# Turned rows and left operands loaded by ScalarE's queue, x and labels by SyncE's, label loads paced

## The reference, cut to what matters

```python
q1 = _attn_pool(x, mask, w1, b1, w2)          # softmax over the 50 rows of exp((x w1 + b1) w2)
q2 = _attn_pool(x, mask, w3, b3, w4)
h = jnp.concatenate([q1, q2], axis=1) @ w5 + b5
f6 = h @ w6 + b6
g = (v @ v.T)[iu, ju]                          # iu, ju: the 44850 pairs i < j
cross = h[:, iu] * h[:, ju] * g
f7 = cross @ w7 + b7
out8 = jnp.concatenate([f6, f7], axis=1) @ w8 + b8
return jnp.einsum('bu,bku->bk', out8, label_embedding)
```

## Time and profile before

| | |
|---|---|
| time, three runs | 1756.97, 1757.58 (median), 1764.65 us |
| profiled execution | 1763.27 us, its span 1761.5 us |
| mean granted TensorE clock | 0.969 of full speed |
| data moved by DMA | 615.20 MB, 349 GB/s over the span |

### The profile page before, as it was taken

The page is one execution under the profiler, slowest core; times in us unless marked ns, Lnnn a source line. Parts: engine busy times, 40 slices in busy tenths (PEclk is TensorE's granted clock), DMA queues, the critical chain, the costliest instruction groups (busy, mean ns, idle before and its releaser), DMA issues.

```text
span 1761.5 us, 25362 instructions
## 1 busy us (share of the span) xinstructions
PE 1580.9 (90%) x7096; PEld 1158.8 (66%) x7096; DVE 1428.3 (81%) x5487; ACT 996.4 (57%) x2931; POOL 138.0 (8%) x96
## 2 busy tenths in 40 slices
PE   1899999999999999999999999989999999997700
PEld 0566677677777777777776777757777777765500
DVE  8997888873898999799997986747777667679966
ACT  7665777765564646464655644434444444433497
POOL 5000000000000000000000000000000000003366
PEclk9999999999999999999999999999999999999955
DMA  7799876977899999999999898999999989999898
GB/s 294 263 401 357 286 274 238 336 268 241 311 329 390 362 400 354 412 374 362 394 355 389 313 389 312 371 414 407 352 379 375 336 309 409 352 356 406 341 397 361
DMA packets 170385, 615.20 MB, mean 349 GB/s; under 512 B 20784, under 2 KB 49421, under 8 KB 162053
## 3 DMA queue, kind: packets, MB, share of 16 engines
q1 hardware_dynamic: 106469, 368.44, 54.8%
q10 hardware_dynamic: 61696, 242.33, 37.0%
q0 software_dynamic: 2080, 2.81, 0.5%
HBM read 609.70 MB, written 3.79 MB: 348 GB/s over the span
## 4 chain that ended last, share of the span: by engine, by line
PE 67%; DMA 14%; DVE 12%; ACT 5%; issue 1%; ACTq 0%; POOL 0%; SPq 0%; DVEq 0%; POOLq 0%
PE bank L704 61%; DMA wring<-in_w7p 8%; DVE stream L1072 4%; DVE cring L1051 3%; DVE junk L951 3%; PE bank L654 2%; DMA stream<-in_label 2%; ACT stream L871 2%; DMA stream<-in_x 2%; PE bank L669 2%; DMA sring<-hrows 1%; ACT absjunk L769 1%; ACT wring L860 1%; ACT stage L871 1%; PE bank L689 1%
## 5 line engine op out<-in xcount | busy, mean ns | idle before, releaser
L704 PE MATMUL bank<-wring,cring 128*128 128x300 f32 (+1 forms) x5616 | 1444.0, 418 | 41.4 <-DVE cring L1051 15.3
L704 PEld LDWEIGHTS bank<-wring,cring 128*128 128x128 f32 (+1 forms) x5616 | 1062.2, 190 | 407.2 <-issue 32.6
L860 ACT ACTIVATE wring<-wring,gcol 128x300 f32<-128x300 f32 x1403 | 655.4, 534 | 675.1 <-PE bank L704 583.5
L1051 DVE TENSOR_TENSOR cring<-lefts,sring 128x1024 f32<-128x1024 f32 (+2 forms) x312 | 371.9, 1192 | 183.3 <-PE bank L704 157.4
L1072 DVE SCALAR_TENSOR_TENSOR stream<-stream,out 128x300 f32<-128x300 f32 x1080 | 441.8, 466 | 0.5 <-DMA stream<-in_label 0.5
L951 DVE SCALAR_TENSOR_TENSOR junk<-stream,ubc 128x300 bf16<-128x300 f32 x784 | 320.1, 466 | 31.9 <-DMA stream<-in_x 31.9
L769 ACT ACTIVATE absjunk<-stream 128x300 bf16<-128x300 f32 x448 | 196.0, 439 | 14.4 <-DMA stream<-in_x 8.9
L654 PE MATMUL bank<-stream,stage 128*32 128x300 f32 x896 | 63.9, 438 | 37.0 <-DVE small L993 36.4
L1072 DVE DVE_READ_ACCUMULATOR stream<-stream,out 128x1 f32 x1080 | 89.0, 82 | 0.0
L769 ACT ACTIVATION_READ_ACCUMULATOR absjunk<-stream 128x1 f32 x448 | 83.9, 187 | 0.0
L1072 DVE SCALAR_TENSOR_TENSOR stream<-stream,bank 128x300 f32<-128x300 f32 x160 | 64.8, 461 | 22.1 <-DMA stream<-in_label 22.1
(11 more groups left out here) (88 smaller groups left out, 516.7 us busy)
## 6 DMA issues: line engine op xcount, KB each, us to landing
wring<-in_w7p ACTq DMA_DIRECT2D x365, 600.0 KB, 7.4
stream<-in_label SPq DMA_DIRECT2D x276, 750.0 KB, 10.1
stream<-in_x SPq DMA_DIRECT2D x64, 1050.0 KB, 11.9
sring<-hrows SPq DMA_DIRECT2D x152, 256.0 KB
stage<-in_label SPq DMA_DIRECT2D x44, 750.0 KB, 9.2
wring<-in_w7p ACTq DMA_DIRECT2D x18, 450.0 KB, 4.6
wring<-in_w7p ACTq DMA_DIRECT2D x18, 300.0 KB, 6.7
sring<-hrows SPq DMA_DIRECT2D x96, 44.0 KB
```

What stands on the lines that cost most here:

```text
L704: mm = pe.matmul(acc[b % 4][:, 0:E], cring[0:rows, p % CSLOTS, b % 2, j0 + j, :], w, start=(p == BEGIN[b] and j == 0), stop=(p == END[b] - ...
L860: ins = nc.scalar.activation(w, w, ACT.Copy, scale=gcol[:, t:t + 1])
L1051: nc.vector.tensor_tensor(cut(cring, p % CSLOTS, j0), in0, cut(sring, nb % SSLOTS, j0), ALU.mult).then_inc(c_ready, 1)
```

## The change

The functions `s_load` and `left_load` move, unchanged but for the engine, from SyncE's program to ScalarE's. On ScalarE `s_load` stands behind `w7_load` and ahead of `w7_scale` in its step, and `left_load` behind `w7_scale`. The loads for the first units, which SyncE had at step 0, stand at the end of ScalarE's step -1. SyncE keeps `x`, labels, constants and the last results. The label plan loses its three-step distance: a new slot is free at once (the four that lie where constants were, at `H_DONE` = 248), and no load is placed less than two steps behind the third load ahead of it. By the code, 32 of the 320 loads get another step: seven early ones move from steps 100 to 105 to 99 to 104, and loads 134 to 158, which stood at 246 to 268, stand at 247 to 267, three in two steps at most.

```diff
-    assert X_DONE + 3 * (FIRST_LATE - NARROW) > DOTS[NS - 1][1] + LATE[H_OUT]
+    H_DONE = DOTS[NS - 1][1] + LATE[H_OUT] + 1
...
         free = (L_END[L_BEFORE[n]] if L_BEFORE[n] is not None else
-                X_WIDE_DONE + n if n < NARROW else X_DONE + 3 * (L_SLOT[n] - NARROW))
-        L_LOAD.append(max(free, L_LOAD[-1] if n else free))
+                X_WIDE_DONE if n < NARROW else H_DONE if L_SLOT[n] >= FIRST_LATE else X_DONE)
+
+        L_LOAD.append(max([free] + L_LOAD[-1:] + [q + 2 for q in L_LOAD[-3:-2]]))
+    assert all(a < z for a, z in zip(L_LOAD, L_END))
...
             for q in range(START, STOP):
-                if q == 0:
-                    s_load(0)
-                    left_load(0)
-                    s_load(1)
                 for n in [n for n in range(XSLOTS, NS * PARTS) if x_load_step(n) == q]:
                     x_load(n)
-                if q == 0:
-                    for n in range(2, SSLOTS):
-                        s_load(n)
-                if 0 <= q < POS:
-                    for n in BUFFERS:
-                        if NU * (n // BUFS) + LAST_USE[n % BUFS] == q and n + SSLOTS in BUFFERS:
-                            sp.wait_ge(c_ready, q + 1)
-                            s_load(n + SSLOTS)
-                    for b in whole(H_OUT, q - STORED):
-                        if b >= 1:
-                            left_load(b)
                 for n in [n for n in range(NBT * LC) if L_LOAD[n] == q]:
                     l_load(n)
...
                 if 0 <= q < POS:
                     if q + WSLOTS - 1 < POS:
                         w7_load(q + WSLOTS - 1)
+                    for n in BUFFERS:
+                        if NU * (n // BUFS) + LAST_USE[n % BUFS] == q and n + SSLOTS in BUFFERS:
+                            act.wait_ge(c_ready, q + 1)
+                            s_load(n + SSLOTS)
                     if q + AHEAD < POS:
                         w7_scale(q + AHEAD)
+                for b in whole(H_OUT, q - STORED):
+                    if b >= 1:
+                        left_load(b)
...
                 if q == -1:
                     for p in range(AHEAD):
                         w7_scale(p)
+                    s_load(0)
+                    left_load(0)
+                    for n in range(1, SSLOTS):
+                        s_load(n)
```

More of the change, by code:

```diff
@@ L451, in l_load @@
                 sp.dma_start(lring[L_SLOT[n]], label_v[n // LC, :, n % LC]).then_inc(l_in[L_SLOT[n]], 16)
[L453 to L506, removed]
@@ L845, in out8_done, with turned, left_load @@
                 act.sem_inc(out8_ready, 1)
+            def turned(b, row, pitch, rows, tiles):
+                return bass.AP(hrows[b].tensor, row * P, [[P, rows], [pitch * P, tiles], [1, P]])
+            def left_load(b):
+                if b >= 4:
+                    act.wait_ge(c_ready, END[b - 4])
+                act.wait_ge(a_stored[b], 16 * 2)
+                for name in ("A32", "A64"):
+                    row = A0 + int(name[1:])
+                    act.dma_start(left_of(name, b), hrows[b][row:row + P]).then_inc(lefta_in[b], 16)
+                act.wait_ge(bc_stored[b], 16 * 4)
+                for name in ("B32", "B64", "B96"):
+                    row = B0 + int(name[1:])
+                    act.dma_start(left_of(name, b), hrows[b][row:row + P]).then_inc(leftb_in[b], 16)
+                four = bass.AP(hrows[b].tensor, C0 * P, [[0, 4], [P, 32], [1, P]])
+                act.dma_start(left_of("C", b), four).then_inc(leftb_in[b], 16)
@@ new lines, in s_load @@
+            def s_load(n):
+                kind, own = KINDS[n % BUFS]
+                s = s_in[n % SSLOTS]
+                for b in live_at(n):
+                    tiles = sring[:, n % SSLOTS, b % 2]
+                    act.wait_ge(a_stored[b], 16 * 2)
+                    if kind != "A":
+                        act.wait_ge(bc_stored[b], 16 * 4)
+                    if kind == "D":
+                        act.wait_ge(d_stored[b], 16 * 2)
+                    if kind in ("A", "B", "D"):
+                        row = {"A": A0, "B": B0, "D": D0}[kind] + QUAD * own
+                        src = bass.AP(hrows[b].tensor, row * P, [[P, P], [1, QUAD * P]])
+                        act.dma_start(tiles.rearrange("p j l -> p (j l)"), src).then_inc(s, 16)
+                        continue
+                    for side in range(2):
+                        j0, ni = 2 * side, CUSTOM[own]
+                        if own == 4:
+                            for r in range(4):
+                                row = C0 + 40 + r + (0 if side else 3)
+                                src = bass.AP(hrows[b].tensor, row * P, [[0 if side else 3 * P, 7], [1, P]])
+                                act.dma_start(tiles[7 * r:7 * r + 7, j0, :], src).then_inc(s, 16)
+                            row = C0 + (0 if side else 22)
+                            act.dma_start(tiles[28:LAST_ROWS, j0, :], hrows[b][row:row + 22]).then_inc(s, 16)
+                            continue
+                        if own == 0:
+                            half = 0 if side else 64
+                            act.dma_start(tiles[0:64, j0, :], hrows[b][A0 + half:A0 + half + 64]).then_inc(s, 16)
+                            act.dma_start(tiles[64:P, j0, :], hrows[b][B0 + half:B0 + half + 64]).then_inc(s, 16)
+                            j0, ni = j0 + 1, 1
+                        i0 = max(0, 2 * own - 1)
+                        for k, (r0, r1) in enumerate(((0, REST), (REST, 2 * REST), (2 * REST, P))):
+                            src = turned(b, C0, 0, r1 - r0, ni) if side else turned(b, C0 + 3 * i0 + 1 + k, 3, r1 - r0, ni)
+                            act.dma_start(tiles[r0:r1, j0:j0 + ni, :], src).then_inc(s, 16)
```

## The result

The changed kernel takes 1845.3 us (median of 4 runs, 1841.8 to 1849.0) against 1760.6 us for the kernel before on the same chip (4 runs, 1757.0 to 1764.7): ratio 1.0475, 95% interval 1.0455 to 1.0495. That is 85 us slower, where 12 to 15 had been forecast. The profiled execution took 1846.9 us, its span is 1845.1 us and its granted clock 0.950 (before: span 1761.5 us, clock 0.969).

What follows compares the result with a forecast made beforehand. The prediction took TensorE to bound the middle and DMA both ends. Its terms, +28.5 - 8.7 - 3 - 2 = +14.8 us, on the 1757.6 us median gave 1772 us, with an 8-in-10 range of 1745 to 1790.

Steps and rivals of the forecast that it cites:

- Together 9.6 + 2.7 + 16.2 = 28.5 us, bounds 0 and 30: Part 1, turned rows issued by ScalarE: TensorE's loss at own0 (9.6), own3 (2.7) and own4 (16.2 us).
- lost one for one: 180 to 1558 us, TensorE-bound: whatever makes TensorE wait costs equal time; some 16 us were to be won.
- own1 and own2: nothing, the cover is thin: Steps loading own1 and own2: 6.9 us of ScalarE work against 8.08, so no loss, with 1.1 us of cover.
- The upper bound of 30: Part 1, issues on ScalarE: the most they could cost, at full issue time, with SyncE's times taken for ScalarE.
- The model of the hold: ScalarE's steps: 5.8 us between weight load and scaling are free, each us beyond is TensorE's; own0 4.4 us each.
- Both alone would do: Hole at 1153 us, step 268: pacing the labels or moving turned rows would each close it, gaining 8.7 us.
- The two medians of the earlier trace: Same 60 us near step 268: label loads landed in 22.9 us, ScalarE's weight loads in 7.8; queues don't hold each other.
- First stage −3: Part 3, tile 0 alone: earlier x loads gain more than late start and own0 cost; 3 us gained, bounds -6 and +4.
- Waits for x −2: Part 4, VectorE's 32.7 us of waits for x: x lands sooner, 2 us gained, bounds -6 and 0.
- hidden issues: Rival: ScalarE's issues cost TensorE nothing, so 1744 us; chance 0.25.
- half the price: Rival: a small piece's issue on ScalarE takes 0.25 us, so 1753 us; chance 0.14.
- ScalarE's queue becomes the late one: Rival: turned rows hold up weights in their shared queue, another 8 to 20 us, 1780 to 1792 us; chance 0.08.

Runs made afterwards that it cites:

- e5: Kernel before with the new label plan and only the own buffers issued by ScalarE, the other turned rows and left operands by SyncE: 1833.0 us, ratio 1.0391.
- e9: Changed kernel with each own buffer loaded as one DMA a tile, 128 runs of 2 KB, other rows of h: 1767.1 us, ratio 1.0027.
- e13: As e9, but each own load split by partitions into 10 or 6 issues a tile, still 2 KB runs: 1836.8 us, ratio 1.0429.
- e16: As e9, with 14, 6 or 12 wasted copies a tile on ScalarE behind each own load, holding ScalarE as long as e13's pieces: 1806.8 us, ratio 1.0260.
- e1: Kernel before with the new label plan alone, turned rows and left operands still on SyncE: 1758.4 us, ratio 0.9988.
- e2: Changed kernel with the old label plan, a burst of 18 label loads in step 268: 1843.9 us, ratio 1.0473.
- e12: Kernel before with the new label plan; GpSimd issues turned rows and left operands between steps 42 and 371, SyncE in the other steps: 1754.7 us, ratio 0.9960.
- e7: Changed kernel with SyncE keeping its old waits for h and for VectorE, empty, so early x loads go out late: 1850.2 us, ratio 1.0493.
- e11: Changed kernel with own buffers and left operands back on SyncE, only kinds A, B, D on ScalarE: 1770.5 us, ratio 1.0047.
- e3: Changed kernel with only the own buffers back on SyncE, kinds A, B, D and left operands on ScalarE: 1782.6 us, ratio 1.0121.
- e10: Changed kernel with at most four own pieces issued a step, spread over three or five steps, same queue: 1816.9 us, ratio 1.0314.

## Why the prediction was wrong

The direction was right and so was its first cause: ScalarE's issues delay the scaling and TensorE waits for it. The size was wrong by a factor of six, outside the range. By the terms of the sum:

- **"Together 9.6 + 2.7 + 16.2 = 28.5 us, bounds 0 and 30" is the step that failed.** The own buffers alone cost 69 us (e5), or 79 against a single load a tile (e9). Three things are missing in it. First the clock: a long hole costs some 2 us more than its wait, and TensorE's busy time rose by 27.5 us in all; I had priced waits alone ("lost one for one"), though the hole of the earlier trace rows, a wait of 8.72, is worth 10.5 when it goes. Second the shared queue: 30 us (e13 less e16), of which weights that land late behind the pieces are the part that rows show; I had left this to a rival. Third the length of the issues where short runs meet full queues: 12.4 and 12.6 us for own1 and own3 in place of 4.7. It is why "own1 and own2: nothing, the cover is thin" failed at steps 124 and 217, 9 and 11 us, and why own3 lost 9.4 us at step 150 in place of 0.9. With long runs these three holes are gone, but two of late weights stand near steps 128 and 221, so that the net is 8 us: the stretched issue and the late weight stand in for each other, and no run parts them.
- The upper bound of 30, hardly above the term itself, was set at the full issue time *as seen on a quiet SyncE queue*. The two issues of the earlier trace rows that took 6.21 us were against it, and so was a row of the trace of before that I passed over, own3's twelve pieces of step 150:

```profile
648.20 20.85 SPq L506 DMA_DIRECT2D sring<-hrows  x12
```

  Taken as the bound (20.85 + 0.38 + 1.85 against 6.06) that step alone would have lost 17 us in place of 0.9, which puts the upper end at 1806 us by this step alone.
- **The model of the hold held.** With matched holds and no pieces in the queue (e16) the holes are 4.56 and 4.42 us at own0 (worked out: 4.4 each), 0.80 us in step 200 with its mixing (worked out: 0.8), 0.88 and 0.95 us at own3 of steps 150 and 336 (worked out: 0.9) and 4.8 us at each of own4's three (3.5, 5.6 and 7.1 were worked out, 5.4 in the mean; that the mean comes near is in part luck).
- **"Both alone would do" was half wrong.** The pacing alone only moves the hole (e1); the queue alone closes it (e2 and the changed kernel, step 277). The gain was 10.5 us, not 8.7. The two medians of the earlier trace rows had it right: what is behind in one queue does not hold the other. The Trainium skill ("DMA: Bandwidth & Descriptors", section "Issuing engines are not separate DMA queues") says that issuing from several engines only saves the sequencer's time. The runs do not agree: another queue closed the hole (e2, ratio 1.0473 against 1.0475 with the pacing), as did GpSimd's (e12), and pacing in the same queue did not (e1, 0.9988); the times of the earlier trace rows run from the issue on, so no sequencer's time is in them.
- **First stage −3:** it lost 13.8 us by step 42. The `x` loads went out at once, three at 62.17 us, and e7 shows 7 us of gain from it. The DMA share from 78 to 178 us fell from 0.98 to 0.89, so the side of the term that counted bandwidth held. The late start is not what failed either: I had taken 2.5 us for it, and at step 1 the kernel is 3.4 us behind. The loss comes behind it. TensorE's waits for scaling between 60 and 200 us rose from 2.1 to 12.8 us, the longest, 4.8 us, at own0 of step 14 (worked out: 2.4). But e9 and e11 lose 10 to 12 us by step 42 with one issue a tile, or with the own buffers on SyncE. What costs them that stays open.

```profile
62.17 1.36 SPq L443 DMA_DIRECT2D stream<-in_x  x3
```

- **Waits for x −2:** VectorE's wait fell from 32.7 us to 8.7, and no time came with it, since TensorE wasn't waiting there.

```profile
DVE junk L948 <- DMA stream<-in_x: 8.7, 5, 3.4
```

Of the rivals, hidden issues and half the price are refuted by the rows of steps 107 and 124. The one that I gave least, "ScalarE's queue becomes the late one", was true as well, on top of the forecast: e13's weights, issued three units ahead, landed in 20.8 us near step 128 and not in 7.8, where e9's took 14.2. I had read its price off the burst of the earlier trace rows, in which there were no pieces in the weights' own queue.

A rival to "the queue" is that the two engines' issues wait for something that both share, since SyncE's issues are long in the same moments (four label loads in 10.49 us from 571.95 us on, in the changed kernel). The kernel before speaks against it. While SyncE's two issues took 6.21 us, those of the weights on ScalarE, six between 1151 and 1172 us (shortest, median, longest in ns), took

```profile
L852 ACTq DMA_DIRECT2D wring<-in_w7p x6: 334/334/367, 1151.3 to 1171.5; - x6
```

What stays open: how the pieces in ScalarE's queue delay the weights behind them, when an issue is stretched and when the load behind is late in its place, and why one load of weights in e9 took 12.12 us to issue. e13's pieces are as large in sum as e9's loads. And the matching of the holds in e16 is good to about 0.6 us a place, so the split of 41 and 30 is no finer than its intervals.

## What to carry to other kernels

Don't put many small DMAs on the queue and the engine that feed the bounding engine: here they cost by the time they held the engine, by loads behind them that came late, and by the clock after each hole. Price an issue by the longest row of its kind, not by one from a quiet stretch, and add the slow microseconds behind a hole to the hole (2 us behind one of 4.4 to 6.9 us here). If one queue holds up another kind of load, an engine with nothing urgent behind the issue is the place for it (e12), and only in the stretches in which it helps.

## What the runs showed of the hardware beyond what I expected

- An issue of a DMA on ScalarE's sequencer takes 0.33 to 0.6 us in most places, and 1 us each for pieces of 512-byte runs in three places of the changed kernel with a DMA share of 1.01 or 1.02; with a share of 1.01 in step 243 it took 0.47. One load of weights took 12.12 us behind six loads of left operands (e9), another 6.84 us (e3), another 5.78 us (e10). In the kernel before no weight load took over 1.35 us.
- The stretch belongs to one engine's queue: 3.1 us an issue on SyncE and 0.33 to 0.37 us on ScalarE in the same 20 us of the kernel before.
- TensorE's granted clock fell from 1.00 to 0.5 within a stand of 6.45 us and came back some 5 us after work did.
- Two kernels with the same bytes and the same issuing engine differ by 70 us by the number of issues alone (e9, e13).
